# First batch's softmax weights transposed by TensorE in fp32 instead of by DMA; their high halves on ScalarE in the later batches; all orders written anew

## The reference

```python
# self-attention, 16 heads of 32, causal
Q, K, V = X @ Wq.T + bq, X @ Wk.T + bk, X @ Wv.T + bv
attn = softmax(where(causal, Q K^T / sqrt(32), -inf))     # (b, h, q, k)
x = layernorm(x + (attn @ V) @ Wo.T + bo)
# cross-attention: one head of 128, its weights between context rows
attention = softmax((ctx @ Wq2.T + bq2) @ (ctx @ Wk2.T + bk2).T)
x = layernorm(x + einsum('bln,bmn->blm', x, attention))
# feed-forward, ternary weights, activations rounded to 8 bits per row
xq = activation_quant(rms_norm(x))
p = silu(xq @ sign(W_g).T) * (xq @ sign(W_u).T)           # hidden 2048
x = layernorm(x + p @ sign(W_d).T)
```

## Time and profile before

| | |
|---|---|
| median of 3 executions | 628.76 us (626.74 to 629.14) |
| the profiled execution | 626.21 us, its span 624.2 us |
| mean granted TensorE clock | 0.964 of full speed |
| busy: PE / DVE / ACT / POOL | 552.5 / 494.7 / 396.3 / 408.1 us |
| DMA queue of SP | 88.1 MB, 70% of 16 engines' span |
| batch 0's last weights-by-values product ends | 146.0 us after the start |
| last PE product ends | 618.4 us after the start |

### The profile page before, as it was taken

How to read it: one execution, slowest core, us unless ns; L and a number is a source line. 1 busy time by engine, 2 the same in 40 slices (tenths; PEclk the granted TensorE clock), 3 DMA queues, 4 the chain that set the end, 5 groups by cost and what they waited for, 6 DMA issues and landing times. The chain is left out here.

```text
span 624.2 us, 14611 instructions
## 1 busy us (share of the span) xinstructions
PE 552.5 (89%) x5532; PEld 352.1 (56%) x5532; DVE 494.7 (79%) x1264; ACT 396.3 (63%) x741; POOL 408.1 (65%) x421
## 2 busy tenths in 40 slices
PE   5996595669999999898989999989989998999996
PEld 4464362347645656465656566567555565575572
DVE  5778654576899878979896877887998889878675
ACT  5899776375578776567567654465776876444151
POOL 1366735578387878768675666765677889846443
PEclk9998598769999999999999999999999999999999
DMA  9899999987366959898852719485295799852000
GB/s 319 318 248 208 241 217 234 242 144 128 69 103 117 193 122 186 162 162 136 145 96 43 149 41 180 77 153 127 50 156 107 121 204 154 144 93 59 18 35 34
DMA packets 241381, 89.55 MB, mean 143 GB/s; under 512 B 227872, under 2 KB 232480, under 8 KB 239776
## 3 DMA queue, kind: packets, MB, share of 16 engines
q1 hardware_dynamic: 240768, 88.11, 70.0%
q10 hardware_dynamic: 544, 0.52, 0.2%
HBM read 27.79 MB, written 4.19 MB: 51 GB/s over the span
## 5 line engine op out<-in xcount | busy, mean ns | idle before, releaser
L1203 POOL TENSOR_TENSOR ph<-p,ph 128x768 f16<-128x768 f32 (+1 forms) x96 | 174.1, 1818 | 69.5 <-ACT ph L793 43.9
L853 ACT ACTIVATE p<-ps_b,tops 128x128 f32<-128x128 f32 (+3 forms) x256 | 119.9, 535 | 51.4 <-DVE tops L1022 27.5
L1022 DVE CUSTOM_DVE_ANT_0 ps_b<-ps_b,future 128x128 f32<-128x128 f32 (+3 forms) x256 | 117.9, 518 | 17.5 <-PE ps_b L682 17.3
L760 PE MATMUL ps_b<-xqT,sg 128*128 128x256 f16 x1024 | 119.7, 273 | 4.5 <-DVE o L1043 1.0
L775 PE MATMUL ps_b<-sd,hp 128*128 128x512 fp8e4 x512 | 118.3, 379 | 2.0 <-DVE gt L1126 1.5
L760 PEld LDWEIGHTS ps_b<-xqT,sg 128*128 128x128 fp8e4 x1024 | 97.2, 98 | 26.4 <-ACT p L853 3.8
L1199 POOL TENSOR_TENSOR hp<-gt,hp 128x512 f16<-128x512 f32 x64 | 76.1, 1196 | 47.6 <-ACT hp L793 47.6
L626 PE MATMUL ps_b<-xhl,wh 128*128 128x256 f16 x480 | 84.9, 276 | 8.0 <-DVE o L1043 4.8
L775 PEld LDWEIGHTS ps_b<-sd,hp 128*128 128x128 f16 x512 | 47.9, 98 | 56.8 <-issue 1.7
L626 PE MATMUL ps_b<-xhl,wl 128*128 128x256 f16 x240 | 66.3, 276 | 0.0
L932 ACT ACTIVATE gt<-gt 128x512 f32<-128x512 f32 x64 | 40.0, 630 | 36.2 <-DVE gt L1121 36.1
(11 more groups left out here) (112 smaller groups left out, 910.9 us busy)
## 6 DMA issues: line engine op xcount, KB each, us to landing
...
pt<-ph SPq DMA_TRANSPOSE x96, 4.3
...
```

What stands on the lines that cost most here:

```text
L760: ins = pe.matmul(ps[:, a * HALF:(a + 1) * HALF], sg[:, ("gg", "uu").index(name), c, ht * P:(ht + 1) * P], xqT[:, c, :], start=c == 0, sto ...
L853: ins = act.activation(p32[:, n % P32_SLOTS, to:to + keys], ps[:, col:col + keys], ACT.Exp, scale=-1.0, bias=tops[:, s % 2, g, j, qt % 2:q ...
L1022: ins = dve.tensor_tensor_reduce(scores, scores, future[:, S - width:S], EXP_SCALE, 3e38, ALU.add, ALU.min, tops[:, s % 2, g, j, qt % 2:qt ...
L1203: pool.tensor_tensor(out_, in_, hi, ALU.subtract).then_inc(signal, 1)
```

## The change

1. **Batch 0 (the first FIRST = 24 pairs): PE transposes.** A new task `tw` on PE transposes the fp32 weights in p32, 128x128 block by block, into PSUM: four blocks fill a bank, so a pair takes two banks (4 + 2 blocks of 768 columns, 4 + 4 of 1024). There are 16 x 6 + 8 x 8 = 160 transposes. `hi` on ACT now copies each bank to the high blocks of pt, `lo` on DVE subtracts and writes the low blocks of pt. For these 24 pairs POOL's `lo`, DVE's `hi`, the buffer ph and the DMA `tp` are gone. p32 is free as soon as the transposes are done.
2. **Batches 1 to 3 (72 pairs):** the DMA transposes as before, but SHARED = 24 too: every high half is made on ACT, and DVE makes none (its edited function is used by no pair).
3. **pt has six slots** instead of five.
4. **The five lists are written anew**, so other tasks are moved as well, and the banks are dealt out anew.
5. A DMA scratch size of the program goes from 4096 to 1024.

```diff
-P32_SLOTS, PH_SLOTS, PT_SLOTS, HP_SLOTS = 3, 3, 5, 6
+P32_SLOTS, PH_SLOTS, PT_SLOTS, HP_SLOTS = 3, 3, 6, 6
+FIRST, SHARED = 24, 24
+TURN_BLOCKS = 4
@@ the lists; two lines of PE_ORDER
-en0.2@5 en0.1@6 en0.0@7 va0.1.0@4 va0.1.1@1 mx0.0.1.0@6,7,2,3 qk0.1.1@4 pv0.0.0.0@5 pv0.0.0.1@5 qk0.1.2@1
+tw0.0.0.0.0@2,1 bv@4 tw0.0.0.0.1@1,0 tw0.0.1.0.0@2,7 tw0.0.1.0.1@4,5 en0.2@3 en0.1@0 en0.0@2 pv0.0.0.0@7 pv0.0.0.1@7
@@ PE
+            def turn_weights(s, g, i, pair):
+                n, blocks = pairs_to(s, g, i, pair), 2 * width_of(s, i) // P
+                wait(pe, p_exp, 0, pieces_to(s, g, HG * i + 2 * pair + 2))
+                wait_for(pe, consts, CONSTS)
+                for j in range(2):
+                    ps = open_bank(("tw", s, g, i, pair, j))
+                    for q in range(j * TURN_BLOCKS, min((j + 1) * TURN_BLOCKS, blocks)):
+                        to = (q - j * TURN_BLOCKS) * P
+                        ins = pe.transpose(ps[:, to:to + P], p32[:, n % P32_SLOTS, q * P:(q + 1) * P], ident[:])
+                    done(ins, ("tw", s, g, i, pair, j))
@@ PE, weigh
-                    wait(pe, turned[n % PT_SLOTS], n // PT_SLOTS, 16)
+                    if n < FIRST:
+                        wait(pe, tw_lo, 0, 2 * n + 2)
+                    else:
+                        wait(pe, turned[n % PT_SLOTS], (n - FIRST) // PT_SLOTS, 16)
@@ ACT, exponentials
-                wait(act, p_lo, 0, n - P32_SLOTS + 1)
+                before = n - P32_SLOTS
+                if 0 <= before < FIRST:
+                    act.wait_ge(*filled("tw", *pair_at(before), 1))
+                elif before >= FIRST:
+                    wait(act, p_lo, 0, before - FIRST + 1)
@@ ACT, p_high
+                if n < FIRST:
+                    pt_free(act, n)
+                    for j, cols, hi, _ in halves_of(n, width):
+                        act.wait_ge(*filled("tw", s, g, i, pair, j))
+                        ps = bank_of("tw", s, g, i, pair, j)
+                        split(hi, ps[:, 0:cols].rearrange("p (q n) -> p q n", n=P), tw_hi.sem)
+                    return
@@ DVE
-                dve.tensor_copy(ph[:, n % PH_SLOTS, 0:width], p32[:, n % P32_SLOTS, 0:width]).then_inc(p_hi[1].sem, 1)
+                weights = p32[:, n % P32_SLOTS, 0:width]
+                dve.tensor_tensor(ph[:, n % PH_SLOTS, 0:width], weights, weights, ALU.max).then_inc(p_hi[1].sem, 1)
+            def turned_low(s, g, i, pair):
+                n, width = pairs_to(s, g, i, pair), 2 * width_of(s, i)
+                for j, cols, hi, lo in halves_of(n, width):
+                    wait(dve, tw_hi, 0, 2 * n + j + 1)
+                    ps = bank_of("tw", s, g, i, pair, j)
+                    low(lo, ps[:, 0:cols].rearrange("p (q n) -> p q n", n=P), hi, tw_lo.sem)
@@ POOL, p_low
-                wait(pool, p_hi[pair], 0, n // 2 + 1)
+                if n < SHARED:
+                    wait(pool, p_hi[pair], 0, (n - FIRST) // 2 + 1)
+                else:
+                    wait(pool, p_hi[0], 0, (SHARED - FIRST) // 2 + n - SHARED + 1)
```

More of the change, by code:

```diff
@@ new lines @@
+mx1.0.0.0@1,2,7,5 dn0.0.0.2@3 xm0.1.0@0 mx1.0.1.0@5,7,2,1 xm0.1.1@4 dn0.0.1.0@5 mx1.0.2.0@1,4,2,7 qk1.1.0@0
+pv1.0.0.0@1 pv1.0.0.1@1 pv1.0.0.2@1 pv1.0.0.3@1 qk1.1.2@4 dn0.0.1.1@5 dn0.0.1.2@5 mx1.0.3.0@0,7,1,2 pv1.0.1.0@6
+pv1.0.1.1@6 qk1.1.3@4 cp1.0@1 cp1.1@2 pv1.0.1.2@6 pv1.0.1.3@6 pv1.0.2.0@4 pv1.0.2.1@4 uu0.0.7@7 pv1.0.2.2@4
+pv1.0.2.3@4 va1.1.0@1 mx1.1.0.0@4,6,7,2 pv1.0.3.0@0 pv1.0.3.1@0 dn0.0.0.3@3 pv1.0.3.2@0 pv1.0.3.3@0 en1.0@4 en1.1@6
+en1.2@7 dn0.0.1.3@5 en1.3@2 ib1@3 uu0.1.0@1 gg0.1.2@6 gg0.1.1@5 gg0.1.0@0 uu0.1.1@4 gg0.1.5@3 gg0.1.4@0 gg0.1.3@5
@@ new lines @@
+uu0.1.3@1 uu0.1.2@4 va1.1.1@2 dn0.1.0.0@6 uu0.1.4@5 mx1.1.0.1@1,2,4,7 dn0.1.0.1@6 dn0.1.1.0@4 mx1.1.1.0@5,7,0,2
+gg0.1.7@3 uu0.1.7@1 uu0.1.5@5 gg0.1.6@7 uu0.1.6@0 op1.0.0@5 pv1.1.0.0@7 pv1.1.0.1@7 pv1.1.0.2@7 pv1.1.0.3@7
+dn0.1.1.1@4 mx1.1.1.1@3,5,0,2 op1.0.1@7 mx1.1.2.0@0,5,3,1 dn0.1.0.2@6 dn0.1.0.3@6 mx1.1.2.1@5,0,2,7 dn0.1.1.2@4
+va2.0.1@1 pv1.1.1.0@2 pv1.1.1.1@2 mx1.1.3.0@7,0,5,6 pv1.1.1.2@2 pv1.1.1.3@2 qk2.0.0@3 mx1.1.3.1@5,2,0,7 dn0.1.1.3@4
+xm1.0.0@3 pv1.1.2.0@2 pv1.1.2.1@2 xm1.0.1@4 pv1.1.2.2@2 pv1.1.2.3@2 mx2.0.0.0@7,0,3,5 va2.0.0@4 qk2.0.2@7 qk2.0.1@3
@@ L286 @@
+hh3.1.5 hh3.1.6 hh3.1.7 dn3.1.0 dn3.1.1
 """
@@ L498, in ph_free, with pt_free, halves_of @@
         def ph_free(eng, n):
-            if n >= PH_SLOTS:
-                wait(eng, turned[(n - PH_SLOTS) % PT_SLOTS], (n - PH_SLOTS) // PT_SLOTS, 16)
+            if n >= FIRST + PH_SLOTS:
+                wait(eng, turned[(n - PH_SLOTS) % PT_SLOTS], (n - FIRST - PH_SLOTS) // PT_SLOTS, 16)
+        def pt_free(eng, n):
+            if n >= PT_SLOTS:
+                s0, g0, _, pair0 = pair_at(n - PT_SLOTS)
+                wait(eng, pv_done, s0, HG * g0 + 2 * pair0 + 2)
+        def halves_of(n, width):
+            blocks = width // P
+            for j in range(2):
+                at, upto = j * TURN_BLOCKS, min((j + 1) * TURN_BLOCKS, blocks)
+                yield j, (upto - at) * P, pt[:, n % PT_SLOTS, at:upto, :], pt[:, n % PT_SLOTS, blocks + at:blocks + upto, :]
         def qk_free(eng, s, g):
@@ L779, in _ @@
             in_order(PE_ORDER, {
-                "qp": first_queries, "qk": project, "va": values, "bv": bias_out, "mx": scores, "pv": weigh,
+                "qp": first_queries, "qk": project, "va": values, "bv": bias_out, "mx": scores, "tw": turn_weights, "pv": weigh,
                 "cp": project_context, "en": energies, "op": project_out, "xm": cross, "ib": spread_steps,
```

384 lines of the change are left out of this document (189 added, 195 removed).

## The result

The changed kernel takes 603.96 us (median of 4 executions, 602.89 to 604.59) against 628.15 us for the kernel before (median of 4, 626.74 to 629.14): the ratio is 0.9615, with a 95% interval of 0.9589 to 0.964. That is 24.2 us less. The profiled execution took 603.64 us.

A forecast was written before the change was run, and what follows sets the result against it. PE, busiest overall, was held in batch 0 by full DMA engines; afterwards ACT would set its end. PE ends at 128 + 472.4 + 2.4 - 1.0 = 601.8 instead of 618.4, so 628.8 - 16.6 = 612 us, range 597 to 630.

The forecast's parts named there:

- End of batch 0: 128: Last weights-by-values product of batch 0: ends at 128 us instead of 146.0, 18.0 earlier.
- The clock, 13.5 us regained: PE in 46.8 to 78.0 and 93.6 to 140.4 us: its work at full clock would take 13.5 us less.
- PE's transposes, 17.6 us: Batch 0 on PE: 160 fp32 transposes at 0.11 us each add 17.6 us at full clock.
- PE's sum, 114: PE up to batch 0's end: 105.6 - 13.5 + 17.6, less 2.4 moved, plus 6.4 free at the start.
- ACT sets the end: Batch 0: ACT's work of 117 us plus 6.9 free at the start puts its last high half at 124.
- the transposes beside megabytes of signs hold ph: Batch 0, 64.5 to 134.9 us: full DMA engines (share 1.05) delay POOL's `lo`; ACT waits 10.0 us, scores 8.1 and 5.6.
- The shift of the high halves at nothing: Batches 1 to 3: ACT gains 33.2 us of high halves, DVE loses 36.2; PE covers both with other tasks' work.
- the new lists leave as much idle as the old: Batches 1 to 3: the old lists leave PE 25.5 us free, and the new ones are assumed to leave as much.
- more is won: Rival, chance 0.15: batch 0 ends at 120, later batches give back 6.3 us, 3 from lighter DVE; 599 us.
- The banks: Rival, chance 0.10, little won: in batch 0 scores wait for banks instead of DMA, 12 us go; 624 us.
- ACT too full later: Rival, chance 0.05, later batches: both high halves stand on ACT's list; half of 33.2 us cancels the gain, all gives 645.
- The transposes run cold: Rival, chance 0.10: clock not regained, batch 0's transposes take 0.27 us each, PE's sum is 153; 637 us.

The follow-up runs named there:

- the whole path for nothing: Kernel before, with POOL's low halves and the transposing DMAs of batch 0 both left out (its output not the reference's): 620.19 us, ratio 0.9889.
- the run in the old lists: Kernel before, with DVE's 36 high halves of batches 1 to 3 made by ACT, each behind its pair's last exponential: 650.74 us, ratio 1.0381.
- the 320: Transposes in the changed kernel with each of its 160 transposes done twice into the same place: 617.04 us, ratio 0.9829.

## Why the prediction was right, and where it was not

The forecast was 612.0 us in a range of 597 to 630, the result 604.0. The direction and the way it comes about were right: batch 0 ends much earlier because PE no longer waits, the clock stays up, and the later batches cover what is moved. It is 8 us too slow, two of its causes fell, and there is luck in the number: its two errors in the kernel's stretches go against each other. The 8 us are 9.6 that the later batches did better, less 3.7 that batch 0's end did worse, and 2.3 between single executions and medians (the profiled one of before was 2.6 us under the median it was put to, that of after 0.3 under its own).

- **End of batch 0: 128, measured 131.7.** The gain there is 14.3 us instead of 18.0.
  - *The clock, 13.5 us regained: measured 8.3.* This is the term that was mis-sized. It multiplied PE's work in two stretches by their mean clock, but PE was idle for much of the low time: its work at the low level was 22.6 us, so no more than 11.3 could come back. And 3.0 are still paid. The second low stretch, 73.5 to 76.9 us, comes after PE had waited 1.72 us for a bank that a low half frees and 0.87 for exponentials.
  - *PE's transposes, 17.6 us: about right.* The row's 22.1 is the time in which a transpose is under way; its ends overlap with other products. From start to the start of the next instruction, waits left out, the 160 take 19.9 us, and 12 of them at the low level are 1.3 of the difference.
  - *PE's sum, 114.* PE is busy for 114.9 us up to the end, where the sum had 107.3, and idle for 16.8, where it had the 6.4 of the start alone. It had no term for waits between 17.8 us and the end, 10.5 us.
  - *ACT sets the end (124 for its last high half): measured 126.4, but as the bound it is refuted.* ACT's work to there is 11.0 + 42.8 + 56.9 = 110.7 instead of 117. The copies explain that: 0.74 for a pair of 768 columns in a full row and 0.96 for one of 1024, where I had 0.99 and 1.23, as the instructions overlap. ACT is idle for 15.7 us instead of 6.9, and taking 13.3 of its work away won 1.6. PE, whose sum I had 10 below ACT's, sets the pace: 19.8 us more work on it put the end off by 18.0 in the profiled execution. From ACT's last high half to the end it is 5.3 us, where I had 2 to 3 for the low half and the products.
  - *DVE's subtractions:* 0.682 and 0.415 us as durations, where the rows of before had 0.685 and 0.425. Right.
- **What held batch 0 before: refuted.** The step "the transposes beside megabytes of signs hold ph" took a DMA share of 1.05 for a bound. A share of 0.78 with few signs, and of 0.44 without the transposes, left batch 0 as it was. What held it was the loop behind the same waits of ACT for POOL: exponential, high half, POOL's low half, three slots of p32; one slot more gives 5.3 us, the whole path for nothing 8.7. The other 5.6 go with the clock that stays up, by the new order, by PE's transposes or by both. The prediction's sum didn't need this step, as it added up each engine's work; so a wrong cause stood under a nearly right number.
- **Batches 1 to 3: 473.8 from batch 0's end to the last product, measured 464.2.** 9.6 us better than forecast. The sixth slot (1.0) measured about that in the medians, but its profile has the gain in batch 0 (144.8) and not here. The shift of the high halves at nothing was wrong in both directions: alone in the old lists it costs some 22 us, undone in the new ones 31 to 40, a part of each in clock. And "the new lists leave as much idle as the old" failed: 16.3 instead of 25.5 us. Together with the shift they leave ACT 7.5 us of waits for maxima instead of 23.5. Against that stand the 4.5 us lost to the low clock, without which these batches would be shorter still. The rival "more is won" had this mechanism, with 3 us for it.
- **Where the later gain sits is settled only so far.** It is not batch 0's transposes (the rest is 460.2 with DMA there, 3.0 of the difference from 464.2 being clock), not the slot alone, not the split alone. Which of the moves in the lists carry it wasn't tried, nor the new lists with five slots.
- **The rivals.** The banks: PE waited 2.3 us for one that a low half frees and 2.7 for exponentials before transposes, not 12. ACT too full later: ACT is busy 318.9 of 464.2 us and POOL waits 37.7 us for its high halves where it had waited 25.8 for ACT's and 15.1 for DVE's; the fear wasn't borne out here, but the run in the old lists shows that it was a real way to lose, at 22 us.
- **The transposes run cold.** Twelve of the 160 did, and 31 of the 320; the others start 0.11 us apart at full clock. PE in the windows before and at the low stretch of the twelve (PE busy, clock, DMA):

```profile
68.00:73.50 5.50, 2.33 (x56) 1.00 0.76 280
73.50:76.90 3.40, 3.30 (x16) 0.50 0.69 133
```

The clock fell after PE had been busy for 2.33 of 5.50 us. It rose after 3.30 us of work, of which 2.82 were transposes. The Trainium skill, "TensorE: Matmul & The Clock Gate", Part 4, has about 275 ns for one transpose and says that the mode doesn't count as activity for the full clock. The 273 ns that the trace gives as the duration of one agrees; as the price of each in a row it doesn't, and the clock here did rise behind a row of twelve transposes, though every row stands between other products, so transposes alone weren't tried. On the choice itself the Trainium skill, "VectorE: DVE Perf Modes", "Rules for kernel authors", says that a 128x128 transpose belongs on TensorE where its result may go to PSUM. The run with the new lists and DMA transposes agrees (40 us slower). In the old lists no run shows it, as leaving the DMAs out altogether was worth 1.5 us of batch 0.
- **The signs in the profile.** Of what the prediction named, the last `v,pt` product (131.7 for 128), the clock (0.98 from 46.8 to 128), the DMA share (0.57), the SP issues (2.0 us at most), ACT's share (92% from 17.8 to 126.4) and the transposes' 0.11 came. The copies' durations were longer than the 0.6 and 0.38 named. The later batches' 474 us didn't. ACT's share came although ACT wasn't the bound: a busy engine isn't one that sets the pace.
